# Re-timing the side work in layers 1 and 2: an earlier second measurement, an earlier weight split, and a bias product moved from the end of a loop to its start

## The reference, cut to what matters

```python
# layer 1: attention of 32 query heads over 8 key heads, then out = out @ Wo + bo and
x = out + hidden_state
return (x - mean(x)) * rsqrt(var(x) + 1e-6) * gamma + beta
# layer 2: x_c is layer 1's result, x_s the context
Mn = conv1x1(Wn, bn, inorm(x_c));  Mm = conv1x1(Wm, bm, inorm(x_s))
A  = softmax(einsum('bct,bcs->bts', Mn, Mm))
Ml = conv1x1(Wl, bl, x_s)
return conv1x1(Wo, bo, einsum('bcs,bts->bct', Ml, A)) + x_c
# layer 3: layer norm, self attention, layer norm, cross attention (16 heads each), layer norm, MLP
```

## Time and profile before

| | |
|---|---|
| time, median of 3 runs | 1873.89 us (1871.45 to 1874.52) |
| time of the profiled execution | 1871.45 us |
| its span | 1869.3 us |
| PE busy | 1715.1 us, 92% of the span |
| DVE, ACT, POOL busy | 51%, 54%, 26% |
| layer 1's attention loop | from 1226 to 1388.5 us |
| layer 2's loop | from 1388.5 to 1495.2 us |

### The profile page before, as it was taken

One profiled execution on the slowest core, in us unless ns is written; L12 is line 12 of the kernel. 1 busy time (PEld: TensorE's weight loads), 2 busy tenths in 40 slices (PEclk: granted clock), 3 DMA queues, 4 the chain that ended last, 5 costly groups with the idle time before them and its releaser, 6 DMA issues. The chain is left out here.

```text
span 1869.3 us, 36312 instructions
## 1 busy us (share of the span) xinstructions
PE 1715.1 (92%) x14357; PEld 1458.4 (78%) x14357; DVE 951.9 (51%) x2096; ACT 1012.1 (54%) x1949; POOL 481.0 (26%) x554
## 2 busy tenths in 40 slices
PE   5999999999978999999999869889989789987698
PEld 4888898888867888888988758756766567776588
DVE  6344444444464444444444463467859747767422
ACT  5555545555424555555455344457648757776443
POOL 5000000000011000000000021047764558766311
PEclk7999999999978999999999879989989999999799
DMA  5000000000011000000000010130010000000001
GB/s 159 24 23 19 3 22 22 22 0 22 1 39 53 1 22 22 22 22 1 22 22 1 1 49 0 29 100 2 2 22 2 1 7 2 2 12 30 1 12 34
DMA packets 58098, 39.84 MB, mean 21 GB/s; under 512 B 14693, under 2 KB 57238, under 8 KB 58006
## 3 DMA queue, kind: packets, MB, share of 16 engines
q1 hardware_dynamic: 58006, 38.57, 7.0%
HBM read 36.46 MB, written 2.10 MB: 21 GB/s over the span
## 5 line engine op out<-in xcount | busy, mean ns | idle before, releaser
L679 DVE TENSOR_TENSOR l0a_c_lo<-l0a_c_ps,l0a_c_hi 128x512 fp32r<-128x512 f32 x128 | 88.6, 692 | 267.4 <-ACT l0a_c_hi L633 267.4
L621 ACT ACTIVATE l0a_weight_t<-l0a_t_ps 64x256 f32<-64x256 f32 x256 | 96.8, 378 | 230.7 <-PE l0a_t_ps L522 229.2
L718 DVE TENSOR_TENSOR x<-l0a_o_ps,x 128x1024 f32<-128x1024 f32 x64 | 78.4, 1224 | 202.8 <-PE l0a_o_ps L102 202.8
L542 PEld LDWEIGHTS l0a_c_ps<-l0a_weight_t,l0a_v 128*128 128x128 f32 x1024 | 135.3, 193 | 14.4 <-ACT l0a_weight_t L621 3.0
L100 PE MATMUL l0a_o_ps<-l0a_wo_hi,l0a_c_hi 128*128 128x256 f32 x512 | 144.2, 282 | 0.0
L101 PE MATMUL l0a_o_ps<-l0a_wo_lo,l0a_c_hi 128*128 128x256 f32 x512 | 143.8, 281 | 0.0
L102 PE MATMUL l0a_o_ps<-l0a_wo_hi,l0a_c_lo 128*128 128x256 f32 x512 | 143.7, 281 | 0.0
L100 PE MATMUL l0a_v_ps<-l0a_wv_hi,ctx_hi 128*128 128x256 f32 x512 | 143.6, 280 | 0.0
L102 PE MATMUL l0a_v_ps<-l0a_wv_hi,ctx_lo 128*128 128x256 f32 x512 | 143.6, 280 | 0.0
L468 POOL COPY l0a_head_bias<-l0a_bias_cols 128x2 f32 (+1 forms) x32 | 6.9, 214 | 531.2 <-DVE l0a_logit L672 531.2
L101 PE MATMUL l0a_v_ps<-l0a_wv_lo,ctx_hi 128*128 128x256 f32 x512 | 143.0, 279 | 0.0
(11 more groups left out here) (430 smaller groups left out, 4871.0 us busy)
## 6 DMA issues: line engine op xcount, KB each, us to landing
l0a_raw<-in_L_xattn_wq_dram SPq DMA_DIRECT2D x32, 128.0 KB, 2.2
l0a_raw<-in_L_xattn_wk_dram SPq DMA_DIRECT2D x32, 128.0 KB, 2.3
l0a_raw_v<-in_L_xattn_wv_dram SPq DMA_DIRECT2D x16, 256.0 KB, 3.0
l0a_raw_o<-in_L_xattn_wo_dram SPq DMA_DIRECT2D x32, 128.0 KB, 2.6
l0a_wo_all<-in_L_xattn_wo_dram SPq DMA_DIRECT2D x2, 2048.0 KB
ctx_rows<-in_ctx_dram SPq DMA_DIRECT2D x4, 512.0 KB, 5.6
x<-in_x_dram SPq DMA_DIRECT2D x4, 512.0 KB, 9.3
l0m_raw<-in_L_xattn_w_fc_dram SPq DMA_DIRECT2D x2, 1024.0 KB, 6.5
```

Of the source, the lines that this page charges most:

```text
L542: last = pe.matmul(by_tile[:, m, b, :, :], v[(j - HP) // HP % 2][:, m * HB + b, p * K:(p + 1) * K], weight_t[:, m, b, :, :].rearrange("p a ...
L621: last = act.activation(weight_t[half, :, :, a, :], t_ps[half, 0:GT // 2 * P] .rearrange("p (m b q) -> p m b q", b=HB, q=SEQ), ACT.Copy)
L679: dve.tensor_tensor(c[p][1][:], c_ps[:], c[p][0][:].bitcast(F32), ALU.subtract).then_inc(c_lo, 1)
L718: dve.tensor_tensor(chip.x[:, rows, :], o_ps[:], chip.x[:, rows, :], ALU.add).then_inc(added, 1)
```

## The change

Three edits. In layer 1 `remeasure`, `regather` and `invert` of a pair stand one slot earlier, and there is one slot less. In layer 2 the eight weight splits start in slots 0 (high) and 2 (low) in place of 2 and 4, and POOL's masks start in slot 10 in place of 14. And the product for `bo_row` moves: ACT's wide copy from slot 16 to slot 0, PE's products from one block in slot 18 to one attention's pair in slot 1 and one in slot 2, DVE's adds to slots 2 and 3. It has no bank of its own there: both use the second half of `out_ps`, so the second product waits for the first add, and the first output product (tile 0, slot 3, same bank) waits for the second add. On DVE the add stands behind the two maxima of its slot.

```diff
-    SLOTS = CHUNKS + LAG + (6 if ending else 3 if following else 2)
+    SLOTS = CHUNKS + LAG + (5 if ending else 3 if following else 2)
...
-                    if restored_pair(s - 3) is not None:
-                        invert(restored_pair(s - 3))
+                    if restored_pair(s - 2) is not None:
+                        invert(restored_pair(s - 2))
...
+                    if restored_pair(s - 1) is not None:
+                        remeasure(restored_pair(s - 1))
                     if restored_pair(s - 2) is not None:
-                        remeasure(restored_pair(s - 2))
-                    if restored_pair(s - 3) is not None:
-                        regather(restored_pair(s - 3))
+                        regather(restored_pair(s - 2))
...
-    HI_SLOT = (2, 3, 5, 7, 9, 11, 13, 15)
-    LO_SLOT = (4, 5, 6, 8, 10, 12, 14, 16)
+    HI_SLOT = (0, 1, 3, 5, 7, 9, 11, 13)
+    LO_SLOT = (2, 3, 4, 6, 8, 10, 12, 14)
...
     def scalar(act, s):
-        if s == NT:
+        if s == 0:
...
-    def tensor(pe, s, bank):
-
-        if s == NT + 2:
-            pe.wait_ge(wide_done, len(phases))
-            for i in PHS:
-                for c in range(CH):
-                    last = pe.matmul(bank[:, i * D:(i + 1) * D], bv_wide[:, i, c, :], raw[i]["o"][:, c, :], start=c == 0, stop=c == CH - 1)
+    def tensor(pe, s, half_ps):
+
+        if 1 <= s <= len(phases):
+            i = s - 1
+            pe.wait_ge(wide_done, i + 1)
+            if i > 0:
+                pe.wait_ge(bo_done, i)
+            for c in range(CH):
+                last = pe.matmul(half_ps, bv_wide[:, i, c, :], raw[i]["o"][:, c, :], start=c == 0, stop=c == CH - 1)
             last.then_inc(bv_made, 1)
 
-    def vector(dve, s, bank):
-        if s == NT + 3:
+    def vector(dve, s, half_ps):
+        if 2 <= s <= len(phases) + 1:
+            i = s - 2
             dve.wait_ge(bo_in, 32)
-            dve.wait_ge(bv_made, 1)
-            for i, ph in enumerate(phases):
-                dve.tensor_tensor(ph["bo_row"][:], bank[:, i * D:(i + 1) * D], ph["bo_row"][:], ALU.add).then_inc(bo_done, 1)
+            dve.wait_ge(bv_made, i + 1)
+            dve.tensor_tensor(phases[i]["bo_row"][:], half_ps, phases[i]["bo_row"][:], ALU.add).then_inc(bo_done, 1)
...
     def gpsimd(pool, s):
-        if s == 14:
+        if s == 10:
...
-        if s in (15, 16):
-            ph = phases[s - 15]
+        if s in (11, 12):
+            ph = phases[s - 11]
...
+                    last["tensor"](pe, n, out_ps[:, D:2 * D])
                     if out:
                         pe.wait_ge(mo_done, n - 2)
                         if n >= 4:
                             pe.wait_ge(out_done, n - 3)
+                        else:
+                            pe.wait_ge(last["bo_done"], 2)
                         pe.matmul(out_ps[:, 0:D], w_cols[:, 3, :], attended[:], start=True, stop=True).then_inc(out_made, 1)
-                    last["tensor"](pe, n, mo_ps)
...
-                    last["vector"](dve, n, mo_ps)
+                    last["vector"](dve, n, out_ps[:, D:2 * D])
```

More of the change, by code:

```diff
@@ L2030, in gpsimd @@
     def gpsimd(pool, s):
-        if s == 14:
+        if s == 10:
             ready_masks(chip, pool, tag, 16, 16, head_pick, side_mask, tensors["head_mask"], tensors["vb"])
-        if s in (15, 16):
-            ph = phases[s - 15]
+        if s in (11, 12):
+            ph = phases[s - 11]
             pool.wait_ge(mask_in, sum(MASK_COUNT))
             pool.tensor_scalar(ph["mask_bias"][:], ph["masks"][:], -1.0, 10000.0, ALU.add, ALU.mult).then_inc(biases_made, 1)
-            pool.wait_ge(biases_made, s - 14)
+            pool.wait_ge(biases_made, s - 10)
             pool.tensor_scalar(ph["masks"][:], ph["masks"][:], score_scale, None, ALU.mult).then_inc(masks_done, 1)
```

## The result

The changed kernel takes 1889.15 us (median of four, 1888.98 to 1891.27); the kernel before, run beside it, 1874.20. The ratio is 1.0087, with a 95% interval of 1.0070 to 1.0103: 16.3 us slower by the ratio, between 13 and 19 (the two medians lie 14.95 apart). The forecast was 1882.3, slower by 8.4 (its sum, 8.75, a little less), with a range up to 1886.5, 12.6 slower. The direction was right, the size was half of what came.

The account below looks back on a forecast made before the run. PE was taken to bound both loops, busy 133.70 of 137.00 us in layer 1 and 53.40 of 57.50 in layer 2. 5.5 + 4.9 - 1.65 = +8.75 us gave a forecast of 1882.3 us, range 1876.0 to 1886.5.

Parts of the forecast that it names:

- Part 4: Layer 2, slots 10 to 12: masks on POOL late by less than a slot, cost 0; rival up to 2.8 us, chance 0.03.
- the half of the rule that speaks of two inputs: Layer 2, rival: low parts with two SBUF inputs contend with POOL's masks, 1.3 us more, chance 0.02.
- Part 1: Layer 1: earlier remeasure delays normalise, 0.66 us for pairs 0 to 3, 1.02 for 4 and 5, plus tail: +5.5.
- 1.15 for the tail: Layer 1's last slots: invert of pair 5 delays pair 6's spread, restore and remeasure, so normalise is 1.15 us late.
- The 0.34 us wait for ScalarE: Layer 1 after pair 5: PE's wait for an ACT copy behind POOL would swallow 0.34 us, leaving 1.7 of 2.0.
- Part 2: Start of layer 2: bo_row products in slots 1 and 2, waits for the adds, and splits: 2.9 + 1.7 + 0.3 = +4.9 us.
- The waits of 1.7: Layer 2, slots 2 and 3: PE waits some 1.7 us each for DVE's add, which stands behind the maxima.
- the 0.3 for the splits: Layer 2's first slots: low parts in slots 2 and 3 leave DVE no idle time before slot 4's maxima, 0.3 us.
- The rival of the clock: Layer 2's start: PE's clock falls in the two new waits, +4 us, time 1886, chance 0.07.
- Part 3: End of layer 2: without the wide copy 0.7 us won, half of PE's product time 0.95 won, together -1.65 us.
- taken up: Two rivals: layer 1's delays absorbed, 1877.1 us, chance 0.12; layer 2's start absorbed, 1877.7 us, chance 0.08.
- not slower: Rival: layer 2's adds done in time and remeasure in DVE's idle time, only the end's gain stands: 1872.2 us, chance 0.08.

Follow-up runs that it names:

- run 1: Only GpSimd's masks moved to slots 10 to 12, on the kernel before: 1878.76 us, ratio 1.0022.
- run 4: The changed kernel with GpSimd's masks back in slots 14 to 16: 1885.81 us, ratio 1.0063 to the kernel before.
- run 6: The changed kernel with slot 10's masks ahead of the context's normalisation on GpSimd: 1888.39 us, ratio 1.0070 to the kernel before.
- run 5: The changed kernel with GpSimd's memset of slot 10 cut into twelve pieces: 1889.82 us, ratio 1.0082 to the kernel before.
- run 9: The kernel before with masks in slots 10 to 12 and VectorE's multiplication of the weights as a tensor_tensor: 1876.13 us, ratio 1.0015.
- run 3: Only the bo_row product moved (wide copy, products, adds), splits and masks as before, on the kernel before: 1878.92 us, ratio 1.0024.
- run 10: Only the bo_row product moved, with VectorE's adds of slots 2 and 3 ahead of the maxima: 1874.61 us, ratio 1.0006 to the kernel before.
- run 11: Only the weight splits two slots earlier, on the kernel before: 1872.91 us, ratio 0.9999.
- run 12: The kernel before, unchanged, timed and profiled once more: 1873.20 us, ratio 1.0004.
- run 8: The kernel before with the wide copy in slot 0 and the bo_row products in slots 16 and 17, in the convolutions' bank: 1872.72 us, ratio 0.9992.
- run 2: Only layer 1's edit (slots, remeasure, regather, invert), on the kernel before: 1884.70 us, ratio 1.0059.

## Why the prediction was right in sign and wrong in size

**The step that failed is Part 4, "Cost 0" for the masks on POOL.** They cost 3.7 us in the trace and 4.1 in time (run 1), and taking them back wins them back (run 4), which alone would have brought the time into the range. Two things went wrong in it. First, it asked only whether GpSimd would be late, found it wouldn't matter, and was right about that (run 6); but lateness wasn't the price. Second, where it weighed contention it took the wrong partner and read the wrong row. It looked at the low parts, and took the one at 1471.4 as lying under the masks, when the memset of 1467.69 had ended at 1470.51. In the kernel before no `tensor_scalar` between SBUF and SBUF met the memset, but for the last 0.02 us of it; that row could show nothing for or against a hold.

What the runs showed in its place: while GpSimd's memset ran, VectorE's `tensor_scalar` between SBUF and SBUF stood still until it ended (3.49, 3.86 and 1.53 us in runs 1, 5 and 9), its reads of PSUM (run 6) and its `tensor_tensor` (run 9) did not. Under GpSimd's `tensor_scalar` of the masks, which reads SBUF, both forms were held, the second multiplication under L2038 and the low part under L2040 (1.21 for 0.67); in run 9 the second `tensor_tensor` of slot 12 was too (1.26 for 0.42).

The Trainium skill (SBUF — State Buffer, Who interferes with whom) says that `copy` and `tensor_scalar` can enter modes that use two ports, that of such an instruction and a GpSimd one the first has the pair shared with GpSimd for its whole length while the other is fully blocked, and that an instruction with two SBUF inputs contends with a GpSimd instruction that reads SBUF, not with one that only writes it. The traces agree on which forms meet which GpSimd work, and for the memsets and L2038 on the length. They don't agree for L2040, whose hold was over 1.2 us before the trace lets it end (1478.91 against 1480.12). And they add that the waiting VectorE did not come in between twelve memsets in a row (3.19 us of them, 3.86 held). The prediction cited the half of the rule that speaks of two inputs, and priced it at 1.3 us with a chance of 0.02. That half did come, as 0.5 us on the low part.

**Part 1, layer 1: +5.5 forecast, +7.5 came.** 0.66 for each of pairs 0 to 3 measured 0.65. 1.02 for pairs 4 and 5 measured 1.04 and 1.05. 1.15 for the tail measured 1.28. The 0.34 us wait for ScalarE was to swallow as much; it became 0.25, so 0.08 was swallowed: ScalarE's work moved with the rest. And 1.61 us are the clock, which the prediction looked for in layer 2's waits only. It fell behind slot 27 in all five traces with a wait of 1.27 to 1.30 us there, and in none of the others. But the same five have a second wait of this length in slot 31, and there it never fell; what makes the difference is not shown.

**Part 2, the start of layer 2: +4.9 forecast, +5.9 came** (6.2 in run 3). The waits of 1.7 are 1.79, the first behind the add as worked out, and run 10 shows the cause by moving the add. The rest is the clock: late to rise in slot 1 in the changed kernel (1.2 us on the scores and the product), fallen behind the first wait in run 3 (1.5 us on the product and the turning). Of the 0.3 for the splits run 11 shows 0.17. The rival of the clock (+4, a chance of 0.07) was right as a mechanism and came in a smaller size, 1.2 to 1.6 us at a time. The prediction took the clock of this place, 1.00, from a stretch that begins at 1419.80; in the kernel before, the clock was still at its lower level until just ahead of the scores of slot 1 (0.78 over 1394 to 1396, in run 12's rows).

**Part 3, the end: -1.65 forecast, -1.33 came**, and -1.58 up to the last turning of the normed rows. In the trace the end's whole gain can be had without the start's waits (run 8).

**The two rivals "taken up" and "not slower"** are out: each wait was handed on in full, and from slot 6 on the start's loss stood unchanged (run 3: 6.82 us behind at slot 6, at slot 8 and at slot 15).

**The sum by parts.** Masks 4.1, layer 1 11.0, `bo_row` 4.5 and splits -0.2 make 19.4 by their ratios, against 16.3 for the whole. The parts are uncertain by 1.7 to 2.6 us each and the whole by 3.1, so the two agree. The traces add up more closely within the loops: 7.45, 6.2 to 5.9, 3.7 and -1.3 are found again in each kernel that has the part. What is not settled is why layer 1's edit alone took 11.0 us where its stage in the trace grew by 7.45. Against the first profile of before, the others start layer 1 between 0.7 us earlier and 3.65 later and lose up to 1.7 in layer 3, and 0.94 us of run 2's trace are the late rise of the clock in layer 2's slot 1 (run 12). I didn't look at whether a shifted start makes the clock fall in other places.

## What to carry to other kernels

Before work on GpSimd is moved, lay its long instructions over VectorE's stream at the new place: here a `tensor_scalar` between SBUF and SBUF that met a memset waited for its end, while reads of PSUM did not, and the time that an engine shows as spare (3.0 us a slot) said nothing of it. Start the memset where VectorE reads PSUM, or where the loop no longer has GpSimd's regular work ahead of it. An instruction put ahead of one that TensorE already waits for costs its whole length each time (0.65 us for each of four pairs here), and a wait can cost again in clock: after waits of 1.3 to 1.8 us up to 1.6 us more in some places here, and nothing in others. Put a side product where TensorE waits anyway and into a bank that is already free, and put its add ahead of the long reductions of its slot.

## What the hardware showed that I had not expected

- Twelve GpSimd memsets in a row, 3.19 us, held VectorE's `tensor_scalar` as one memset of 2.82 us did (3.86 and 3.49 us for a pair that takes 0.62).
- The granted clock fell to its lower level after a single wait of 1.27 to 1.30 us, in a stretch in which TensorE was otherwise busy, some 2 us after work had resumed, and cost 1.6 us, in slot 27 of five traces; after a second wait of this length in slot 31 of the same five it did not, nor after waits of 0.89.
- GpSimd's `tensor_scalar` of 128x1024 that stands at 2.80 us in the trace held VectorE only in its beginning: a low part that came 0.38 us behind its start took 1.21 us for 0.67, and multiplications that came 1.3 us behind it took their usual 0.61.
- The same code of layer 2's slot 1 took 0.93 us longer in run 1 than in both executions of the kernel before, by the moment at which the clock rose.
